# Attention of a vision-transformer tower: in TensorE's slots the scores of the next exponential are issued ahead of the two projection pieces

## The reference

```
h = tokens(x) @ W + b, with cls_tok in front            # 64 x 197 x 192
# attention, on x = layernorm(h); fq = round, clip to 16 levels, scale back
qkv = fq(x) @ fq(ww1).T                                  # 3 x 12 heads x 64
dots = einsum('bhnd,bhmd->bhnm', fq(q), fq(k)) * 64**-0.5
a = softmax(dots)
out = einsum('bhnm,bhmd->bhnd', fq(a), fq(v))
h = h + fq(out) @ fq(ww2).T + bb2
# feed-forward, on layernorm(h)
h = h + bitlinear(silu(gate) * up), with up, gate = split(bitlinear(x))
```

## Time and profile before

| | |
|---|---|
| median of 3 runs | 1193.98 us (1191.64 to 1194.19) |
| the profiled execution | 1195.78 us, span 1194.0 us |
| busy over the span | PE 1108.2 us (93%), DVE 1056.6 (88%), ACT 923.6 (77%), POOL 466.1 (39%) |
| granted clock of PE, mean | 0.988 of full speed; 1.00 in every stretch read from 220 to 840 us |
| chain that ended last | PE 73%, ACT 10%, issue 7%, DMA 3%, DVE 3% |
| busy in 300 to 800 us, each 100 us | PE 98.0 to 98.4, ACT 97.6 to 98.1, DVE 95.4 to 97.7 |

### The profile page before, as it was taken

One profiled execution on the slowest core, in us unless ns is written; L12 is line 12 of the kernel. 1 busy time (PEld: TensorE's weight loads), 2 busy tenths in 40 slices (PEclk: granted clock), 3 DMA queues, 4 the chain that ended last, 5 costly groups with the idle time before them and its releaser, 6 DMA issues.

```text
span 1194.0 us, 32030 instructions
## 1 busy us (share of the span) xinstructions
PE 1108.2 (93%) x11210; PEld 674.9 (57%) x11210; DVE 1056.6 (88%) x2028; ACT 923.6 (77%) x1832; POOL 466.1 (39%) x498
## 2 busy tenths in 40 slices
PE   7999999889999999999999999999867888888887
PEld 6999998445555555555555555555534444444444
DVE  7687666599999999999999999999887999999996
ACT  0000001889999999999999999999637999999997
POOL 5644344302211223221111232221236777766774
PEclk9999999999999999999999999999879999999999
DMA  8998998445655566556555655555532333333332
GB/s 292 313 314 249 316 306 236 137 138 150 152 150 150 131 147 156 145 150 150 145 150 147 141 150 151 149 151 143 146 98 64 105 101 101 103 99 99 99 95 71
DMA packets 157284, 187.87 MB, mean 157 GB/s; under 512 B 42864, under 2 KB 118464, under 8 KB 156928
## 3 DMA queue, kind: packets, MB, share of 16 engines
q1 hardware_dynamic: 115680, 156.92, 42.2%
q0 software_dynamic: 15936, 10.88, 9.4%
q10 hardware_dynamic: 25536, 18.31, 4.8%
HBM read 143.11 MB, written 36.12 MB: 150 GB/s over the span
## 4 chain that ended last, share of the span: by engine, by line
PE 73%; ACT 10%; issue 7%; DMA 3%; DVE 3%; POOL 2%; SPq 1%; ACTq 1%; DVEq 0%; POOLq 0%
PE psum L1139 14%; PE psum L1197 12%; PE psum L1260 12%; PE psum L1230 7%; PE psum L1200 7%; PE psum L1213 6%; PE psum L1247 6%; PE psum L1326 5%; ACT yi L674 3%; ACT zi L682 2%; ACT big L667 2%; PE psum L1306 1%; PE psum L1316 1%; DMA big<-xt 1%; POOL big L797 1%
## 5 line engine op out<-in xcount | busy, mean ns | idle before, releaser
L1075 DVE TENSOR_TENSOR pi<-big 128x2364 int16<-128x2364 f32 (+1 forms) x128 | 333.8, 2608 | 13.5 <-DMA big<-z_row 13.0
L769 POOL DMA_DIRECT2D h_res<-att x128 | 146.8, 1301 | 492.7 <-ACT att L601 484.0
L625 ACT ACTIVATE big<-psum 128x788 f32<-128x788 f32 (+1 forms) x384 | 330.3, 862 | 5.1 <-PE psum L1247 2.8
L587 ACT ACTIVATE qki<-psum 128x394 int16<-128x394 f32 x384 | 172.4, 508 | 25.5 <-PE psum L1200 13.8
L1139 PE MATMUL psum<-big 128*128 128x192 f32 (+1 forms) x1128 | 185.0, 327 | 2.3 <-DMA big<-xt 2.0
L1139 PEld LDWEIGHTS psum<-big 128*128 128x128 f32 (+1 forms) x1128 | 180.3, 188 | 5.5 <-DMA big<-xt 2.6
L1260 PE MATMUL psum<-big,sa_hot 128*32 128x197 f32 (+1 forms) x3072 | 168.2, 336 | 0.6 <-DVE zt L1099 0.6
L587 ACT ACT_TABLE_LOAD x1 | 1.3, 1283 | 189.5 <-PE psum L1200 189.5
L797 POOL TENSOR_TENSOR big<-big,goutb 128x512 f32<-128x512 f32 (+1 forms) x99 | 123.8, 1270 | 59.5 <-DVE big L1042 59.4
L1247 PE MATMUL psum<-qkb 64*128 64x197 bf16 (+1 forms) x1536 | 128.9, 246 | 1.3 <-DVE qkb L860 1.3
L596 ACT ACTIVATE vi<-psum 128x384 int16<-128x384 f32 (+1 forms) x256 | 115.7, 529 | 4.0 <-PE psum L1200 3.7
(11 more groups left out here) (109 smaller groups left out, 1812.6 us busy)
## 6 DMA issues: line engine op xcount, KB each, us to landing
big<-z_row SPq DMA_DIRECT2D x192, 394.0 KB, 5.0
big<-xt SPq DMA_DIRECT2D x98, 384.0 KB, 4.7
tin<-h_res SPq DMA_DIRECT2D x49, 192.0 KB, 3.0
tres<-h_res SPq DMA_DIRECT2D x49, 192.0 KB, 2.5
out<-oo SPq DMA_DIRECT2D x49, 192.0 KB, 2.6
h_res<-big ACTq DMA_DIRECT2D x84, 96.0 KB, 4.5
h_res<-att POOLq DMA_DIRECT2D x64, 96.0 KB, 3.4
x_int<-big ACTq DMA_DIRECT2D x84, 64.0 KB, 4.4
```

Source lines behind the costliest of these rows:

```text
L587: act.activation(qki[:, k, :, :], psum[:, bank, 0:2 * N] .rearrange("p (c n) -> p c n", c=2), ACT.Copy, scale=factor[(F_Q, F_K)[b % 2]])\
L625: act.activation(ex[0:r, tri, t, 4 * g:4 * g + 4, :].rearrange("p (a h) n -> p a h n", a=2), psum[0:r, 2 * t:2 * t + 2, 0:2 * N] .rearrang ...
L769: pool.dma_start(h_res[bass.ds(b - 4, 1), t0:t0 + r, :].rearrange("a n d -> (a n) d"), att[0:r, par, t, :], accum_op=ALU.add).then_inc(s_a ...
L1075: v.tensor_tensor(pi[0:r, t, :, 0:N], ex[0:r, it, t, :, :], zb[0:r, ip, :, :], ALU.mult).then_inc(s_pi, 1)
```

## The change

In slots 0 to 4 of PE the call of `scores` is issued ahead of the call of `projections`. No matmul, no wait and no semaphore is added or taken away. The lists of the other engines are the same.

```diff
                 if u < 5:
+                    scores(b, par, u)
                     projections(b, u)
-                    scores(b, par, u)
                 if u % 2 == 0:
                     sums(b, tri, u)
                 else:
```

## The result

The changed kernel takes 1217.61 us (median, 1214.96 to 1221.99), the kernel before 1194.09 beside it: ratio 1.019, 95% interval 1.0158 to 1.0222. It is slower, by 23.5 us where 18 were forecast. In a second set of runs the ratio was 1.0182 (1.0144 to 1.0219). The profiled execution took 1216.16 us, span 1214.4, so 20.4 us more than the profiled execution of before.

What follows compares the result with a forecast made beforehand. PE and ACT, handing pieces to each other in a 10.08 us step, were taken as the bound; +0.28 and +0.04 a step over 57 steps give 18.2 us, with +0.4 and -0.4 about +18: median 1212 us, range 1199 to 1219.

Steps and rivals of the forecast that it cites:

- A: Stretch from slot 1's 64-row projection pass to slot 4's, paced by ACT: 4.94 us, to grow by 0.04.
- B: Stretch from slot 4's 64-row projection pass to slot 1's in the next step, PE's own work: 5.13 us, to become 5.41.
- The cover: PE's work ahead of a waiting projection isn't larger: each gap holds one scores and one sums or weighted values either way.
- The price of a change of shape: On PE, each change of the weights' shape costs 0.09 us; six more a step, 0.5 us of PE's time.
- S to P1: On PE, start of scores to start of the projection's 128-row pass: 0.27 to 0.29 us, bounds 0.18 and 0.30.
- O to S: On PE, start of output projection to start of scores: 1.09 us, against 1.00 from output projection to the 128-row pass.
- P2 to Z or W: On PE, the projection's 64-row pass to sums or weighted values, start to start: 0.26 us, bounds 0.17 and 0.28.
- the early steps: Steps 0 to 3, and the v slots of step 62, pay a few gaps as well: +0.4 us.
- Covered waits: Rival: scores fill PE's waits in slots 2 and 4, DVE's 9.76 us sets the pace: -18 us, 1176; chance 0.03.
- Unseen pairs without a gap: Rival: next weights load behind running matmuls: 1190, chance 0.05; with only one kind of pair free 1200, chance 0.08.
- All gaps paid: Rival: waits hide nothing since ACT is delayed as much: 0.64 us a step, 36 us, 1230; chance 0.05.

Runs made afterwards that it cites:

- slot 1 alone: Scores ahead of the projection in slot 1 only, against the kernel before: 1211.33 us, ratio 1.0148.
- slots 2 and 4: Scores ahead of the projection in slots 2 and 4 only, against the kernel before: 1188.98 us, ratio 0.9943.
- slot 4 alone: Scores ahead of the projection in slot 4 only, against the kernel before: 1189.03 us, ratio 0.9947.
- slot 0: Scores ahead of the projection in slot 0 only, against the kernel before: 1208.05 us, ratio 1.0105.
- the exchanged passes: Changed kernel with the projection's 64-row pass ahead of its 128-row pass in slots 0, 1 and 3: 1200.35 us, ratio 1.0036 to the kernel before.
- the old early steps: Changed kernel with the old order of scores and projections in steps 0 to 3: 1216.06 us, against 1218.83 for the changed kernel beside it.

## Why the prediction was right

**The bound.** One cycle of two sections, A at ACT's pace and B at PE's, was right. What moves into B costs in full (slot 1 alone +0.27 us a step), what moves within A costs next to nothing (slots 2 and 4 against slot 4 alone), what leaves B is won in full (slot 4, -0.17). With slot 0, +0.22, the three single slots add up to +0.32; section A grew by 0.04 (4.98 for 4.94), which makes 0.36 of the 0.37 measured for all five. Slot 3 by itself was not run.

**The cover.** "Not larger" was right for the change as a whole: P1 to P2 in slots 2 and 4 is 0.56 us where it was 0.57. It holds because all slots change alike. With slot 4 alone two units of scores stand between P2 of slot 3 and P1 of slot 4, and then the wait is filled.

**The price of a change of shape.** Right in kind and confirmed by the exchanged passes. Shape here is the way the array is divided; between 69 and 128 columns of weights nothing is lost (P2 to S is 0.18 with scores of 69 columns, 578.18 to 578.36, and with 128, 579.87 to 580.05, in the kernel before). Of the pairs that the trace of before didn't have, S to P1 came out at 0.27 to 0.30 (forecast 0.27 to 0.29) and O to S at 1.09 as forecast. **The term that was mis-sized is P2 to Z or W**: 0.26 forecast, 0.27 to 0.28 measured (579.61 to 579.88, 586.38 to 586.66), at its upper bound. It stands twice in section B, which took 5.46 for 5.41 us: 0.03 to 0.04 of that is the two pairs, 0.01 is P1 to P2 of slot 0 (0.44 for 0.43), the rest rounding. At 0.05 a step this is 2.9 us over the 57 steps.

**The sum.** Step 10.44 for 10.39. The stretch grew by 20.5 us where 18.2 - 0.4 = 17.8 were forecast; its start came 0.5 us later (forecast 0.4 for the early steps), and what follows it was 0.6 us shorter. So the profiled execution is 1216.2 for 1214. The median missed 1212 by 5.6 us; the other 3.3 us or so are a choice of mine: I took the median to lie 1.8 below the profiled execution, as it did before, and it lay 1.4 above. Such an offset is chance, since single executions differ by several microseconds. It is luck, too, that the median isn't further off: 1217.61 lies 1.4 us inside the upper end of 1199 to 1219, above the 1207 to 1217 that the forecast itself had, and two of the four executions (1219.06 and 1221.99) lie above both.

**The rivals.** Covered waits (1176) needed all 0.58 us of waits filled and no gap added: the second wait of slots 2 and 4 stayed, and PE lost time in section B. Unseen pairs without a gap (1190 or 1200) failed at the rows: P2 to Z is 0.27, not 0.17, and S to P1 0.27 to 0.30, not 0.18. All gaps paid (1230) would have been 0.64 us a step: the part hidden in section A is real, since PE's waits in front of P1 of slots 2 and 4 went. The rule of the Trainium skill, "TensorEngine Tiling (Array Packing)", Key Properties, that a change of tiling mode drains TensorE, agrees with all pairs seen, with the size above. The reading by which weight loads go unseen to the background buffer (the Trainium skill, "TensorE: Matmul & The Clock Gate", step-by-step on LDWEIGHTS) holds in this case's traces between matmuls of one shape only: the load of P1 starts 0.08 us ahead behind O, and nothing is lost there. That the load isn't taken ahead where the shape changes is shown (0.01 us ahead of its matmul or less); whether a drain is what holds it back no run here tells.

## What to carry to other kernels

When small matmuls of different weight shapes share TensorE, keep those of one shape together: count the changes of shape in an order before moving anything, at 0.09 us each here, and look in the timeline of the weight loads for those that start ahead of their matmul. When two engines hand work back and forth, find the sections of the cycle and who paces each; the same edit is worth +0.27, 0 or -0.17 us a step depending on the section, so apply it slot by slot. Here the edit in slot 4 alone beats both kernels, by 0.5% under the kernel before.

## What was not expected

The busy share of PE rose from 98% to 100% in the kernel that does the same work more slowly, and the longer early steps (9.53 us for 8.54) cost nothing. The chain of the changed kernel that ended last runs there through transfers and not through PE (5.61 us of `big<-z_row` from 244.78 us on, then DVE, before the scores at 253.89). With the old early steps PE reaches that place sooner and waits there, 2.71 us, for DVE. Also the ends of two executions, of the same instructions behind attention, differ by as much (3.7 us) as a small edit is worth.
